# The order of the calls inside a pass, rewritten on four engines of a two-layer transformer and state-space kernel

## Time and profile before

| | |
|---|---|
| Median of three runs | 4406.98 us (4402.31 to 4415.19) |
| Profiled execution | 4410.43 us, its span 4408.7 us |
| TensorE busy in the span | 3700.5 us, 84% |
| VectorE busy | 3558.4 us, 81% |
| ScalarE busy | 2435.4 us, 55% |
| GpSimd busy | 2530.8 us, 57% |
| Mean granted TensorE clock | 0.919 |
| DMA, mean | 56 GB/s |

### The profile page before, as it was taken

How to read it: one execution, slowest core, us unless ns; L and a number is a source line. 1 busy time by engine, 2 the same in 40 slices (tenths; PEclk the granted TensorE clock), 3 DMA queues, 4 the chain that set the end, 5 groups by cost and what they waited for, 6 DMA issues and landing times. The chain is left out here.

```text
span 4408.7 us, 51342 instructions
## 1 busy us (share of the span) xinstructions
PE 3700.5 (84%) x17261; PEld 2188.9 (50%) x17261; DVE 3558.4 (81%) x3917; ACT 2435.4 (55%) x3413; POOL 2530.8 (57%) x1895
## 2 busy tenths in 40 slices
PE   5688888989899898989888898989989898998623
PEld 3364544636464554636464463646455463646301
DVE  4514788979898887989888897989889898988795
ACT  2344555647565565646555564656556564655532
POOL 0131756648484755758474674848475574847462
PEclk8697999999999999999999999999999999999856
DMA  4630211203030110203020120303011020302000
GB/s 176 228 106 1 78 34 39 77 6 111 1 101 15 63 53 25 92 6 111 1 90 27 38 78 6 111 1 101 15 63 53 26 90 6 111 1 87 15 5 5
DMA packets 69436, 247.79 MB, mean 56 GB/s; under 512 B 9600, under 2 KB 10112, under 8 KB 68736
## 3 DMA queue, kind: packets, MB, share of 16 engines
q1 hardware_dynamic: 66816, 235.28, 16.1%
q10 hardware_dynamic: 2304, 8.39, 0.5%
HBM read 212.19 MB, written 31.46 MB: 55 GB/s over the span
## 5 line engine op out<-in xcount | busy, mean ns | idle before, releaser
L668 POOL TENSOR_TENSOR kept<-kept,hb 128x512 f32<-128x512 f32 x640 | 809.5, 1300 | 28.2 <-DVE hb L1821 28.2
L1812 DVE TENSOR_TENSOR_SCAN hb<-ps,hb 128x512 f32<-128x512 f32 x640 | 741.8, 1203 | 6.5 <-ACT ps L1332 5.6
L636 POOL TENSOR_TENSOR kept<-kept,hb 128x1024 f32<-128x1024 f32 x128 | 334.8, 2632 | 698.1 <-DVE hb L1756 639.1
L881 PE MATMUL ps<-hid_bhi,wring 128*128 128x512 f32 x1536 | 623.2, 406 | 17.3 <-issue 13.8
L881 PE MATMUL ps<-hid_blo,wring 128*128 128x512 f32 x1536 | 608.0, 396 | 0.0
L1332 ACT ACTIVATE ps<-kept,a_neg 128x512 f32<-128x512 f32 x640 | 431.7, 691 | 263.3 <-DVE hb L1812 263.3
L621 POOL TENSOR_SCALAR_AFFINE_SELECT room<-room 128x512 f32<-128x512 f32 x256 | 237.8, 945 | 570.8 <-ACT room L1498 570.8
L1882 DVE TENSOR_REDUCE room<-ps 128x4 f32<-128x2048 f32 (+3 forms) x256 | 375.6, 1488 | 234.1 <-PE ps L1060 232.8
L881 PE MATMUL ps<-hid_ahi,wring 128*128 128x512 f32 x1280 | 514.4, 402 | 18.7 <-POOL hid_alo L683 17.9
L881 PE MATMUL ps<-hid_alo,wring 128*128 128x512 f32 x1280 | 503.5, 393 | 0.0
L1498 ACT ACTIVATE room<-ps 128x2048 f32<-128x2048 f32 (+1 forms) x192 | 305.3, 1590 | 256.7 <-PE ps L1086 256.1
(11 more groups left out here) (188 smaller groups left out, 7580.5 us busy)
## 6 DMA issues: line engine op xcount, KB each, us to landing
wring<-w_hi SPq DMA_DIRECT2D x352, 512.0 KB, 3.3
kept<-in_wffn SPq DMA_DIRECT2D x22, 512.0 KB, 6.0
w_hi<-wring SPq DMA_DIRECT2D x22, 512.0 KB, 6.9
w_lo<-wrest SPq DMA_DIRECT2D x22, 512.0 KB, 3.9
xn<-in_x_fm SPq DMA_DIRECT2D x17, 512.0 KB, 3.5
out_fm<-xc ACTq DMA_DIRECT2D x16, 512.0 KB, 5.1
room<-in_wmod SPq DMA_DIRECT2D x2, 1536.0 KB, 8.2
win<-in_win SPq DMA_DIRECT2D x1, 1024.0 KB, 8.4
```

The lines of the kernel that those rows point to most:

```text
L636: pool.tensor_tensor(pair_of(acc, h), pair_of(acc, h), pair_of(hb, h), ALU.add).then_inc(tail_acc, 2)
L668: pool.tensor_tensor(acc[:, m, :], acc[:, m, :], hb[:, s % 8, :], ALU.add).then_inc(acc_done, 1)
L881: mm = pe.matmul(bank(bk), wring[:, r % 3, at + k * P:at + (k + 1) * P], src[i][:, k, :], start=(k == 0 and i == 0), stop=(k == K - 1 and ...
L1812: dve.tensor_tensor_scan(hb[:, s % 8, :], bank(2 + m % 2), hb[:, s % 8, :], 0.0, ALU.mult, ALU.add).then_inc(scanned, 1)
```

## The change

The four lists of calls are put into another order. No call is added or dropped, and no call's waits, signals, tiles or instructions change; some `split` calls of the first pass are merged or stand elsewhere. Below is the diff, with the indentation of the calls taken off.

```diff
@@ -698,89 +698,89 @@
 tail_add(0, 0)
 tail_add(0, 1)
 tail_add(1, 0)
+causal_probs(0, 0)
 tail_add(1, 1)
-causal_probs(0, 0)
+causal_probs(0, 1)
+causal_probs(0, 2)
 tail_add(2, 0)
 tail_add(2, 1)
-causal_probs(0, 1)
-causal_probs(0, 2)
+tail_add(3, 0)
+tail_add(3, 1)
+spread_sums(0)
 causal_probs(1, 0)
-tail_add(3, 0)
-spread_sums(0)
-tail_add(3, 1)
 causal_probs(1, 1)
+make_u(0)
+make_u(1)
 causal_probs(1, 2)
 causal_probs(2, 0)
-make_u(0)
-make_u(1)
+spread_sums(1)
+head_add(0, 0)
 causal_probs(2, 1)
-spread_sums(1)
+head_add(0, 1)
 causal_probs(2, 2)
-head_add(0, 0)
-head_add(0, 1)
-spread_sums(2)
 quant_at(0, 3)
 causal_probs(3, 0)
+spread_sums(2)
+quant_at(0, 12)
 causal_probs(3, 1)
+quant_at(1, 3)
 causal_probs(3, 2)
-quant_at(0, 12)
 spread_sums(3)
+quant_at(1, 12)
 head_add(1, 0)
 head_add(1, 1)
-quant_at(1, 3)
-quant_at(1, 12)
+times_b(2, 3)
 split_h(0)
 split_h(1)
-times_b(2, 3)
+times_b(3, 3)
 add(2, 0)
+add(2, 1)
 split_hid(0)
-times_b(3, 3)
-add(2, 1)
+times_b(4, 3)
 split_hid(1)
-times_b(4, 3)
+add(3, 0)
 split_hid(2)
 split_hid(3)
 split_hid(4)
 split_hid(5)
 split_hid(6)
 split_hid(7)
-add(3, 0)
 add(3, 1)
+add(4, 0)
 split_hid(8)
-add(4, 0)
 times_b(5, 3)
 add(4, 1)
+split_hid(9)
+add(5, 0)
+split_hid(10)
 times_b(6, 3)
-split_hid(9)
-split_hid(10)
+add(5, 1)
 split_hid(11)
-add(5, 0)
-add(5, 1)
 add(6, 0)
-times_b(7, 3)
 split_hid(12)
 split_hid(13)
+times_b(7, 3)
 split_hid(14)
+add(6, 1)
 split_hid(15)
-add(6, 1)
 times_b(8, 3)
 add(7, 0)
 add(7, 1)
+times_b(9, 3)
+add(8, 0)
 split_hid(16)
-times_b(9, 3)
 split_hid(17)
-add(8, 0)
 split_hid(18)
 add(8, 1)
 split_hid(19)
+split_hid(20)
 add(9, 0)
 times_b(10, 3)
-split_hid(20)
+split_hid(21)
 add(9, 1)
-split_hid(21)
+times_b(11, 3)
 split_hid(22)
 split_hid(23)
-times_b(11, 3)
 add(10, 0)
 add(10, 1)
 add(11, 0)
@@ -1133,149 +1133,149 @@
 project(1)
 head_var(0)
 head_var(1)
+tail_spread(1, 0)
 project(2)
 project(3)
 head_var(2)
-tail_spread(1, 0)
+tail_spread(0, 1)
 head_var(3)
-project_v(0)
 gate_in(0)
 pre_var()
 scores(0, 0)
-tail_spread(0, 1)
 gate_in(1)
 scores(0, 1)
-project_v(1)
+project_v(0)
+gate_in(2)
 scores(0, 2)
-gate_in(2)
+gate_in(3)
+tail_spread(1, 1)
 turn_max(0)
-gate_in(3)
 scores(1, 0)
-tail_spread(1, 1)
 in_proj(0)
 scores_turned(0, 0)
 in_proj(1)
+tail_spread(0, 2)
 scores(1, 1)
-tail_spread(0, 2)
 in_proj(2)
 scores_turned(0, 1)
-in_proj(3)
+project_v(1)
 scores(1, 2)
+tail_spread(1, 2)
 values(0, 0)
 scores_turned(0, 2)
-tail_spread(1, 2)
+in_proj(3)
 turn_max(1)
 scores(2, 0)
+values(0, 1)
 tail_spread(0, 3)
+scores_turned(1, 0)
 x_proj()
-scores_turned(1, 0)
-values(0, 1)
-values(0, 2)
+tail_spread(1, 3)
 scores(2, 1)
 dt_proj(0)
-tail_spread(1, 3)
+dt_proj(1)
+values(0, 2)
+dt_proj(2)
 scores_turned(1, 1)
+dt_proj(3)
+scores(2, 2)
 row_sums(0)
-dt_proj(1)
-dt_proj(2)
-scores(2, 2)
+scores_turned(1, 2)
+turn_max(2)
 turn_sums(0)
-dt_proj(3)
-scores_turned(1, 2)
-values(1, 0)
-turn_max(2)
-values(1, 1)
+head_spread(0, 0)
 scores(3, 0)
 out_proj(0)
+values(1, 0)
 scores_turned(2, 0)
+values(1, 1)
 out_proj(1)
 scores(3, 1)
+head_spread(1, 0)
+values(1, 2)
 fin_mean()
-head_spread(0, 0)
-values(1, 2)
 scores_turned(2, 1)
 row_sums(1)
+scores(3, 2)
 fin_var()
-scores(3, 2)
+head_spread(0, 1)
 turn_sums(1)
-head_spread(1, 0)
 scores_turned(2, 2)
+values(2, 0)
+values(2, 1)
+turn_max(3)
 fin_turn(0)
-values(2, 0)
-turn_max(3)
-values(2, 1)
+fin_turn(1)
 values(2, 2)
-head_spread(0, 1)
 row_sums(2)
 scores_turned(3, 0)
+scores_turned(3, 1)
+scores_turned(3, 2)
+fin_back(0)
 turn_sums(2)
-scores_turned(3, 1)
 values(3, 0)
-scores_turned(3, 2)
-fin_turn(1)
+att_proj(0)
 values(3, 1)
-att_proj(0)
+values(3, 2)
 head_spread(1, 1)
-values(3, 2)
 att_proj(1)
 row_sums(3)
 att_proj(2)
 turn_sums(3)
-fin_back(0)
 att_proj(3)
+fin_back(1)
+ffn_mean()
+spread(1, 2)
 spread(0, 2)
-ffn_mean()
 ffn_var()
+fin_ff(0)
 spread(0, 3)
-fin_back(1)
-spread(1, 2)
-fin_ff(0)
 fin_ff(1)
 up(0)
 up(1)
 up(2)
+spread(1, 3)
+spread(0, 4)
 up(3)
 up(4)
-spread(1, 3)
-spread(0, 4)
 up(5)
 up(6)
 up(7)
 spread(0, 5)
 mid(0)
+spread(1, 4)
 mid(1)
-spread(1, 4)
 mid(2)
 spread(0, 6)
+spread(1, 5)
 mid(3)
 mid(4)
-spread(1, 5)
+spread(1, 6)
+mid(5)
 spread(0, 7)
-mid(5)
-spread(1, 6)
 mid(6)
 mid(7)
 spread(0, 8)
+spread(1, 7)
 mid(8)
-spread(1, 7)
 mid(9)
 spread(0, 9)
+spread(1, 8)
 mid(10)
-spread(1, 8)
+spread(0, 10)
 mid(11)
 mid(12)
-spread(0, 10)
 spread(1, 9)
 mid(13)
+spread(0, 11)
 mid(14)
 spread(1, 10)
-spread(0, 11)
 mid(15)
+spread(1, 11)
+next_mean()
 mid(16)
-next_mean()
-spread(1, 11)
+next_var()
 mid(17)
-next_var()
 
         def scalar_pass(act, p):
 b, att, fin, pre, ffn, first = p.b, p.att, p.fin, p.pre, p.ffn, p.first
@@ -1554,147 +1554,147 @@
 square(1)
 head_rstd(0)
 head_rstd(1)
+pre_square()
+square(2)
 odd_version(0)
-square(2)
+square(3)
 odd_version(1)
-square(3)
 head_rstd(2)
 head_rstd(3)
-pre_square()
-copy_v(0)
 odd_version(2)
 odd_version(3)
 split(1, 2, 3, 4, 5, 6, 7, 8)
 pre_rstd()
+tail_decay(1, 0, 1, 2, 3)
 gate_silu(0)
-tail_decay(1, 0, 1, 2, 3)
 gate_silu(1)
+pre_affine()
 gate_silu(2)
-pre_affine()
 gate_silu(3)
+tail_decay(2, 0, 1, 2, 3)
+exp_probs(0, 0)
 copy_xp(0)
-exp_probs(0, 0)
+copy_v(0)
 split(9, 10)
-tail_decay(2, 0, 1, 2, 3)
 copy_xp(1)
-copy_xp(2)
 exp_probs(0, 1)
 copy_v(1)
 split(11)
+copy_xp(2)
+exp_probs(0, 2)
+split(12, 13, 14)
 tail_decay(3, 0, 1)
 copy_xp(3)
-exp_probs(0, 2)
-split(12, 13, 14)
+exp_probs(1, 0)
 tail_decay(3, 2, 3)
 copy_xd()
-exp_probs(1, 0)
+copy_bc()
 dt_bias(0)
-copy_bc()
+dt_bias(1)
 copy_out(0)
 split(15, 16)
+dt_bias(2)
 exp_probs(1, 1)
 split(17)
-dt_bias(1)
-dt_bias(2)
+dt_bias(3)
+softplus()
 exp_probs(1, 2)
 split(18, 19, 20)
-dt_bias(3)
-softplus()
-exp_probs(2, 0)
-skip(0)
 head_decay(0, 0, 1)
 head_decay(0, 2, 3)
-copy_out(1)
+exp_probs(2, 0)
 split(21)
-fin_square()
-exp_probs(2, 1)
-fin_rstd()
+skip(0)
 skip(1)
 skip(2)
+head_decay(1, 0, 1)
+copy_out(1)
+exp_probs(2, 1)
+fin_square()
+skip(3)
+fin_rstd()
+exp_probs(2, 2)
 fin_affine()
-exp_probs(2, 2)
 fin_rows(0)
-skip(3)
 copy_out(2)
-head_decay(1, 0, 1)
 exp_probs(3, 0)
 exp_probs(3, 1)
+fin_rows(1)
 exp_probs(3, 2)
 head_decay(1, 2, 3)
 copy_out(3)
-fin_rows(1)
+decay(2, 0)
 copy_b(2)
 ffn_square()
+fin_cols()
 ffn_rstd()
-decay(2, 0)
-fin_cols()
+decay(2, 1)
 ffn_affine()
-decay(2, 1)
 copy_b(3)
+decay(3, 0)
 up_gate(0)
 up_gate(1)
-decay(3, 0)
 round_up(0)
 up_gate(2)
+copy_b(4)
+fin_bias(0)
 round_up(1)
-fin_bias(0)
 up_gate(3)
 round_up(2)
 up_gate(4)
-copy_b(4)
 decay(3, 1)
 up_gate(5)
 round_up(3)
-fin_bias(1)
-up_gate(6)
 round_up(4)
 round_up(5)
+up_gate(6)
 up_gate(7)
 round_up(6)
 round_up(7)
 decay(4, 0)
+fin_bias(1)
 copy_b(5)
+decay(4, 1)
 gelu(0)
+decay(5, 0)
 gelu(1)
-decay(4, 1)
-decay(5, 0)
+decay(5, 1)
+gelu(2)
 copy_b(6)
-gelu(2)
-decay(5, 1)
+decay(6, 0)
 gelu(3)
-copy_b(7)
-decay(6, 0)
 decay(6, 1)
 gelu(4)
+copy_b(7)
 gelu(5)
+decay(7, 0)
 gelu(6)
-decay(7, 0)
+decay(7, 1)
+copy_b(8)
 gelu(7)
-copy_b(8)
-decay(7, 1)
+gelu(8)
 decay(8, 0)
-gelu(8)
+gelu(9)
 copy_b(9)
+decay(8, 1)
 store_y()
-decay(8, 1)
-gelu(9)
 decay(9, 0)
 gelu(10)
+copy_b(10)
+gelu(11)
 decay(9, 1)
-gelu(11)
-copy_b(10)
 gelu(12)
 decay(10, 0)
-rotate_c()
+copy_b(11)
 gelu(13)
 decay(10, 1)
+decay(11, 0)
 gelu(14)
-copy_b(11)
 gelu(15)
-decay(11, 0)
 decay(11, 1)
 next_square()
 next_rstd()
+rotate_c()
 rotate_b()
 
         def vector_pass(dve, p):
@@ -1955,36 +1955,36 @@
 split(0)
 tail_in(0, 0)
 tail_in(0, 1)
+pre_centre()
 tail_scan(0, 0)
 tail_scan(0, 1)
 normalise(0)
+tail_out(0, 0)
+tail_out(0, 1)
 normalise(1)
-pre_centre()
+tail_in(1, 0)
 normalise(2)
 normalise(3)
 split(1)
-tail_out(0, 0)
-tail_out(0, 1)
+tail_in(1, 1)
 find_max(0, 0)
 split(2)
-tail_in(1, 0)
+pre_scale()
 find_max(0, 1)
 split(3)
-tail_in(1, 1)
+tail_scan(1, 0)
 find_max(0, 2)
 split(4)
-pre_scale()
+tail_scan(1, 1)
 shift_q(0)
 split(5)
-tail_scan(1, 0)
+tail_out(1, 0)
 find_max(1, 0)
 split(6, 7)
-tail_out(1, 0)
-tail_scan(1, 1)
 tail_out(1, 1)
+tail_in(2, 0)
 find_max(1, 1)
 split(8, 9)
-tail_in(2, 0)
 tail_in(2, 1)
 tail_scan(2, 0)
 find_max(1, 2)
@@ -1999,119 +1999,117 @@
 tail_in(3, 0)
 tail_in(3, 1)
 tail_scan(3, 0)
-tail_scan(3, 1)
-find_max(2, 1)
-split(14)
 tail_out(3, 0)
 split_bc()
+find_max(2, 1)
+split(14, 15)
+tail_scan(3, 1)
 tail_out(3, 1)
-invert(0)
-split(15)
 gate_out(0)
 find_max(2, 2)
-weigh(0)
+invert(0)
 split(16)
 gate_out(1)
 gate_out(2)
+clip_dt()
+gate_out(3)
 shift_q(2)
 split(17)
-gate_out(3)
 find_max(3, 0)
-split(18, 19)
-clip_dt()
+weigh(0)
+split(18, 19, 20)
+head_in(0, 0)
 out_add(0)
+head_in(0, 1)
+head_scan(0, 0)
 out_add(1)
 find_max(3, 1)
-split(20)
+split(21)
+head_out(0, 0)
 fin_centre()
-head_in(0, 0)
-head_in(0, 1)
 invert(1)
-split(21)
-head_scan(0, 0)
+head_scan(0, 1)
 find_max(3, 2)
+head_out(0, 1)
 fin_scale()
-head_out(0, 0)
+head_in(1, 0)
 weigh(1)
-head_scan(0, 1)
-head_out(0, 1)
+head_scan(1, 0)
 quant_at(0, 0, 1, 2)
 shift_q(3)
-head_in(1, 0)
 invert(2)
-head_scan(1, 0)
```

(62 more changed lines are left out.)

## The result

The changed kernel takes 4522.69 us (median of 4 runs, 4505.55 to 4534.18), the kernel before 4409.71 beside it: ratio 1.0252, 95% interval 1.0224 to 1.028. It is 113 us slower; the forecast was 4378, 29 us faster. The profiled execution took 4505.55, the lowest of the four, with a span of 4503.8 against 4408.7. The difference of the two spans, 95.1, lies as follows: passes 2 to 14 (thirteen of them, from project(0) of pass 2 to that of pass 15) +80.2, pass 0 +4.6, pass 1 −0.6, ahead of them +0.4, all behind +10.5. That last part still holds pass 15, the fourteenth steady one: from its project(0) to the first pick_mod of pass 16 it is 4.6 longer, and what is behind that 5.9.

What follows compares the result with a forecast made beforehand. TensorE's matmuls were taken to bound the feed-forward half, a queued chain of dependent calls the attention half. −0.7 and −1.4 make −2.1 us per steady pass, 14 times −29, so 4378 us; range 4325 to 4432.

Steps and rivals of the forecast that it cites:

- the walk: Hand-traced start times of the new order through one steady pass, using durations from the earlier trace; result −2.1 us per pass.
- Quad 3: Attention's last quad: out_proj and values calls ahead of chain links make shift_q(3) 5.7 us late, exp_probs(3,2) 3.4 late.
- Into the feed-forward: From attention's end to up(0): ffn_centre 4.4 us late, yet up(0) only 0.45 late because quantisation is already done.
- the chain: Attention half: scores, find_max, turned scores, exp, next scores through four shared PSUM banks; 85 us unhindered, against 102.
- Outside them 0, bounds −8 and +8: Passes other than the 14 steady ones: no change, bounds from 2 us for each of four passes.
- The payback into the feed-forward: Between ffn_centre and up(0): the +4.4 us delay shrinks to +0.45, both pairs being quantised and turned back earlier.
- the delay is not paid back: Rival, chance 0.15: up(0) stays 4.4 us late through GpSimd queueing, a pass loses 1.9 us, total 4434 us.
- mid(0): Feed-forward's first mid stage: three TensorE waits for split_hid, 1.19 us in all, shrink; the eighth split ends 1.0 earlier.
- End of a pass: mid(15) to project(0): reordered norm calls gain 1.4 us despite a new 1.2 us stall of next_mean for gelu(15).
- GpSimd's copy: In spread_sums: 0.60 us alone, 2.61 beside a VectorE scan; (1) and (3) would now meet scans, sum unchanged.
- The chain is not delayed: Rival, chance 0.2: queueing in attention is overstated, up(0) comes 4 us early, −6.1 per pass, total 4322 us.
- No change: Rival, chance 0.2: stalls only move within a pass, waiting for gelu(15) eats the gains, total about 4400 us.

Runs made afterwards that it cites:

- e4: Changed kernel plus eight unread 512-column constant matmuls per steady pass, in four TensorE gaps of the attention half; 4421 us, 102 us less than the changed kernel.
- e7: Changed kernel plus the same eight constant matmuls per steady pass, only 16 columns wide; takes back 1 us of the 113 us loss.
- e14: Changed kernel plus ten constant matmuls per pass, two of them behind ffn_mean, where they overwrite unread data; 26 us slower than the version with eight.
- e9: Changed kernel with softplus and clip_dt put back behind exp_probs(1,2) and weigh(0); 14 us faster than the changed kernel, within the noise.
- e6: Changed kernel plus only the two pairs of constant matmuls after scores_turned(3,0) and (3,1); gives back 31 us where 43 were forecast.
- e5: Kernel before plus eight constant matmuls per steady pass, after scores(3,2), scores_turned(3,0), ffn_mean and ffn_var; 0.27% faster than the kernel before.

## Why the prediction was wrong

**The step that failed is the walk's assumption about TensorE, in "Quad 3" and "Into the feed-forward".** The walk took its durations from rows of before, mostly at the upper clock, and put TensorE's long calls (out_proj, att_proj) and its waits for exp in front of the links of the chain. It had no term for the granted clock: what it is behind those waits, and what the long calls take at it. Forecast and measured shifts against before (medians), in us:

```
                       forecast   after   e4 (clock held up)
exp(1,2)                 +1.95     +1.7      +1.7
shift_q(3)               +5.7      +8.2      +5.3
exp(3,2)                 +3.4      +6.2      +2.8
ffn_centre               +4.4     +11.7      +4.8
up(0)                    +0.45     +8.4      +1.4
```

With the clock held up, the walk holds to a microsecond at each step. Without, shift_q(3) is 2.5 too late, and the step from exp(3,2) to ffn_centre, forecast as "that distance plus 1", took 5.5 more. How the 80.2 us divide isn't shown. Low grew by 104.5 us, and if a matmul at half the clock cost its own lengthening and nothing else, that would be 52 at most; the rest would be low time that the old order bore off the chain and the new one has on it. But low time can also cost more than half of itself: e4's four passes with 0.95 in the stretch have 3.4 us more of it than its usual pass, and up(0) comes 2.9 to 3.8 later in them. The earlier trace rows had shown 0.95 and 0.89 for before; the prediction used the 0.89 to explain one slow fin_ff and never asked what the new gaps would do to it.

The Trainium skill (page "TensorE: Matmul & The Clock Gate", "What's actually happening") says that the throttled state is the default and activity releases it; e4 against e7 agrees (1.00 and 0.86). The Trainium skill (the same page, "Terms") prices a time at the lower clock at its length times the missing share. Half of each microsecond is what that makes here, an estimate from the Trainium skill's page; the runs have 0.32 us for each in the new order and 0.05 to 0.08 in the old, and e4's four passes about 1, so it fits none of them.

**"Outside them 0, bounds −8 and +8"** was too small as well, if by little: what lies ahead of pass 2 came to +4.4 and what lies behind pass 15 to +5.9, together about +10.

**The payback into the feed-forward: right.** From ffn_centre to up(0) took 15.2 before and 11.5 after, median inside a pass: −3.7, forecast −3.95. That is the rival "the delay is not paid back" refuted in its mechanism: its time (4434) was the nearest, but it wanted head_add, times_b and split_h to queue on GpSimd. The delay was paid back; it was nearly three times as large as forecast (11.7 against 4.4).

**mid(0): the gain came, and was lost in front of it.** Of the waits of the earlier trace rows less is left: the first matmul of mid(0) to that of mid(1) went from 5.7 to 4.1, −1.6 (forecast −1.0). But up(0) to mid(0) grew from 16.8 to 18.4 where 0.45 less was forecast, so mid(1) comes 22.5 us after up(0) in both kernels. This is the failed step once more: the first up() runs at the lower clock (0.98 for the whole stage) and up(1) comes 3.3 us after it, 2.27 before. e4's fillers stand ahead of that place and don't help there (18.3); in one of its steady passes and in e14's eight that low stretch is missing, and mid(0) comes after 16.9.

**End of a pass: right in the changed kernel.** The end of mid(15) to project(0) took 16.3 in eleven of passes 2 to 14 against 17.8 in ten of them before, −1.5 (forecast −1.4), next_mean waiting 1.21 us for gelu(15) as forecast 1.2. The gains that the forecast named are there, −3.7 −1.6 −1.5; they stand against +11.7 and the +1.6 ahead of mid(0). In e4's pass 7, where the clock was up there too, the forecast's pass can be seen: 247.6 us, for "about 248".

**GpSimd's copy.** GpSimd's spread_sums(1) and (3), and VectorE's scans beside them, in the changed kernel:

```profile
1204.40 2.55 POOL L628 COPY room<-room 128x512 f32<-128x512 f32 x1 [9.65 <-DVE room L1896]
...
1240.11 2.48 POOL L628 COPY room<-room 128x512 f32<-128x512 f32 x1 [9.61 <-DVE room L1896]
```

```profile
1204.25 2.29 DVE L1776 TENSOR_TENSOR_SCAN hb<-hb 128x1024 f32<-128x1024 f32 x1
...
1239.96 2.23 DVE L1776 TENSOR_TENSOR_SCAN hb<-hb 128x1024 f32<-128x1024 f32 x1
```

Both stand beside a scan and take 2.5 instead of 0.60, as the prediction had it.

**The other rivals.** "The chain is not delayed" is refuted (+8.2 at shift_q(3)). "No change" is what the new order comes to in steady passes once TensorE is kept busy in both (3260.7 against 3262.6), not what it comes to by itself.

**What stays open.** Which gap the extra low time starts from: making the wait of 2.13 us 0.9 shorter moved the time by 14 us, within the noise (e9), filling the two waits in quad 3 gave 31 (e6), and no reordering removed more than 24. That wide fillers help by the clock and not by the 2 us that they take up is read from the durations (att_proj 1.99 for 3.14) and the granted clock; no run has the delay without the work. Fillers in passes 0 and 1 weren't tried, so the 20 us that e4 lies above e5 outside the steady passes aren't explained.

## What to carry to other kernels

A walk through a new order needs TensorE's clock as a term: mark every new wait of TensorE in a stage whose granted clock is already below 1.00, and price the long calls behind it once at the upper and once at the lower clock, as two bounds. To test for it, put matmuls of constants into the gaps, with narrow ones as the control; if the wide ones give the time back, the loss goes with the clock and not with the queues alone. And of a reordering that is meant to pay back a delay, look first at the size of the delay.

## What the runs showed of the hardware that was not expected

Work that nobody reads made a kernel faster: in e5 by 0.27% (interval 0.17 to 0.37), in e4 by 102 us against the changed kernel, with the clock of the stretch from shift_q(2) to up(0) at 1.00 instead of 0.86. The same number of instructions with 16 columns did nothing for it. Behind two waits of 2.00 us the four matmuls of an att_proj ran at a granted clock of 0.50 and took 3.14 us; at 1.00, five microseconds later, they took 1.88.
